# Gated linear attention with experts: output transposes and k transposes at other places in TensorE's order

## The chip, the core and the metric

The kernel runs on one core of one Trainium2 chip. The metric is the device time of one execution in microseconds. Three runs of the kernel before are shown; the changed kernel is compared with it on the same chip.

## The reference

Sixteen sequences of 512 tokens with 256 features go through an attention block and then a feed-forward block with eight experts, each with a layer norm before it, another behind it and a residual:

```
q, k = heads(x@Wq) * HK**-0.5, heads(x@Wk);  v = heads(x@Wv)     # 4 heads, HK = 64, HV = 128
g = log_sigmoid(x@gk_w1@gk_w2 + gk_b) / 16
S = exp(g_t)[:, None] * S + k_t[:, None] * v_t[None, :];  o_t = q_t @ S     # scan over tokens
o = o * rsqrt(mean(o*o) + eps) * rms_w * silu(x@Wg);  return o @ Wo
x = x + layernorm(attn(layernorm(x)))
x = x + layernorm(gelu(layernorm(x)@w1[e] + b1[e]) @ w2[e] + b2[e])          # expert e = sequence // 2
```

## The kernel before

The scan is done in four chunks of 128 tokens (`NCH`). Within a chunk, seven levels of pairwise products (`level`, `top_level`, lines 274 to 308) fill the chunk's attention matrix `Am`; between chunks a state `S` is carried. Projections run as three products of fp32r parts (hi x hi, hi x lo, lo x hi: `three`, lines 262 to 272); transposes, state products and attention products are plain fp32.

The program is a loop over sequences. `run(s, j, e, B, C, A)` does three things in one turn, interleaved by hand: stage B is the attention of sequence s, C is the feed-forward block of sequence p = s - 1, A (with V) is the layer norm, the transposes and the projections of sequence n = s + 1. There is a first fill, a first turn without C, fourteen turns with all three, a turn without A, and a last one with C alone. Each engine has its own copy of this loop and works off its instructions in the order in which they are written; semaphores tie the engines together. So the order inside `run` on each engine is what counts.

The steps of TensorE that the change touches, with `c` for the chunk:
- `xt` transposes the normed x of sequence n into the banks `PT[0]`, `PT[1]`; `x_hi` (ScalarE) and a `lo_part` (VectorE) split them to `xT_hi`, `xT_lo`.
- `kh(f)` (line 389) transposes `k_decayed`, six 128x128 blocks in all, into `PT[f]`; ScalarE copies them to `kT` (`ac_kt`).
- `f2(c)` (line 378) is the second feed-forward product, 24 passes for one chunk; `gd` and `gl` are the products of the gate of sequence n; `kp`, `qp`, `vp(c)`, `gp(c)` are the projections to k, q, v and output gate, each three passes over each half of the features, 6 in all. `vp(1)` waits until ScalarE has copied `v` of chunk 0 (`v_evac(0)`).
- `st(c)` (line 486) is k^T v of a chunk into the bank `PS`; `att(c)` (line 502) is the chunk's output into `PO`, from `Am` and, past the first chunk, from the state.
- `ogt(c)` (line 520) transposes the gated output `o` of a chunk, four blocks, into `PT[c % 2]`. `og_hi(c)` (ScalarE) and `og_lo(c)` (VectorE, line 763) split it to `ogT_hi`, `ogT_lo`. `wo(c)` (line 530), 12 passes, multiplies by Wo into `PL[c % 2]` and needs both.

Between `att(c)` and `ogt(c)` lies a chain over three engines: `o_evac(c)` copies `PO` to `o` (ScalarE), `squares(c)` sums its squares by head (ScalarE, eight short instructions), `o_rstd(c)` takes the reciprocal root (POOL, lines 1384 and 1387), `og(c)` multiplies by it and by the gate (VectorE, line 756).

Three ends of the order matter. TensorE: `ogt(0)` stands between `vp(0, n)` and `gp(0, n)`, `ogt(1)` between `vp(1, n)` and `wo(0)`. VectorE: `og_lo(0)`, `og(1)`, `state(2)`. ScalarE: `squares(1)`, `og_hi(0)`, `v_evac(0, n)`, `o_evac(2)`. In the trace, line 279 is `transpose_tokens`, 398 `kh`, 430 and 432 `gd`, 497 `st`, 513 and 516 `att`, 527 `ogt`, 269 to 271 the three passes of `three`, 693 `lo_part`, 751 `state`, 760 `og`.

Of the kernel before, what the change touches and what calls it, by code (L numbers as in the profile page):

```python
# [21 lines left out]
def build(nc, x_d, wq_d, wk_d, wv_d, wg_d, w1g_d, w2g_d, gkb_d, wo_d, rms_d,  # L22
# [6 lines left out]
    P = 128  # L29
# [9 lines left out]
    KT = D // P  # L39
# [12 lines left out]
    with ctx:  # L52
# [133 lines left out]
        def at(name, b, c):  # L186

            return b * PER[name] + c
# [74 lines left out]
        def _(pe):  # L263
# [19 lines left out]
            def run(s, j, e, B, C, A):  # L283
# [92 lines left out]
                def f2(c):  # L376
                    pe.wait_ge(sem["po_w2"], at("po_w2", e, 8))
                    if c >= 2:
                        pe.wait_ge(sem["dv_y4"], at("dv_y4", p, c - 1))
                    else:  # L380
                        pe.wait_ge(sem["ac_gelu"], at("ac_gelu", p, FT - 1 + c))
                    t = slice(c * CH, (c + 1) * CH)
                    for m in range(FT):
                        pe.wait_ge(sem["dv_hlo"], at("dv_hlo", p, m + 1))
                        last = three(PB[c % 2][:, 0:D], [(h_hi[:, m, t], h_lo[:, m, t])],
                                     [(W2[0][:, m, :], W2[1][:, m, :])], m == 0, m == FT - 1)
                    last.then_inc(sem["pe_f2"], 1)

                def kh(f):
                    pe.wait_ge(sem["po_ku"], at("po_ku", s, 2 * (NL - 1)))  # L390
                    if A:
                        pe.wait_ge(sem["dv_xlo"], at("dv_xlo", n, f + 1))
                    elif C:
                        pe.wait_ge(sem["dv_hlo"], at("dv_hlo", p, FT - 1 + f))
                    for c in range(2 - f):
                        for tl in range(KT):
                            w = (2 * f + c) * CH
                            last = nc.tensor.transpose(PT[f][:, c * D + tl * P:c * D + (tl + 1) * P],
                                                       kk[:, tl, w:w + CH], ident[:, :])
                    last.then_inc(sem["pe_kt"], 1)  # L400

# [57 lines left out]
                def vp(c, b):  # L459
                    if c == 0 and b == 0:  # L460
                        pe.wait_ge(c_lo, 2)
                        pe.wait_ge(sem["k_sb"], at("k_sb", b, 1))
                    elif c == 0:
                        pe.wait_ge(sem["k_sb"], at("k_sb", b, 1))
                    elif c == 1 and b == 0:
                        pe.wait_ge(sem["dv_gl"], at("dv_gl", b, KT))
                        pe.wait_ge(sem["ac_abs"], at("ac_abs", b, KT))
                    elif c == 2:
                        pe.wait_ge(sem["dv_q"], at("dv_q", b, 2 if b else 4))
                    else:  # L470
                        pe.wait_ge(sem["v_sb"], at("v_sb", b, c))
                    token_tile(PL[0] if c == 1 and b == 0 else PB[0], c, 0).then_inc(sem["pe_v"], 1)

                def gp(c, b):
                    if c == 0 and b == 0:
                        pe.wait_ge(c_lo, 3)
                        pe.wait_ge(sem["dv_q"], at("dv_q", b, 4))
                    elif c == 0:
                        pe.wait_ge(sem["k_sb"], at("k_sb", b, 2))
                    elif c == 2 and b:  # L480
                        pe.wait_ge(sem["dv_q"], at("dv_q", b, 4))
                    else:
                        pe.wait_ge(sem["ac_g"], at("ac_g", b, c))
                    token_tile(PB[1], c, 1).then_inc(sem["pe_g"], 1)

                def st(c):

                    pe.wait_ge(sem["ac_kt"], at("ac_kt", s, c // 2 + 1))
                    pe.wait_ge(sem["v_sb"], at("v_sb", s, c + 1))
                    if c:  # L490
                        pe.wait_ge(sem["dv_st"], at("dv_st", s, states(c)))
                    elif C:
                        pe.wait_ge(sem["dv_st"], at("dv_st", p, states(NCH - 1)))
                    for tl in range(KT):
                        for hh in range(2):
                            hd = 2 * tl + hh
                            last = nc.tensor.matmul(PS[hh * HK:(hh + 1) * HK, tl * HV:(tl + 1) * HV],
                                                    kT[:, c, hd * HK:(hd + 1) * HK],
                                                    v[:, c, hd * HV:(hd + 1) * HV], start=True, stop=True)
                    last.then_inc(sem["pe_st"], 1)  # L500
# [19 lines left out]
                def ogt(c):  # L520
                    pe.wait_ge(sem["dv_og"], at("dv_og", s, H * (c + 1)))
                    if c >= 2:
                        pe.wait_ge(sem["dv_oglo"], at("dv_oglo", s, c - 1))
                    else:
                        pe.wait_ge(sem["ac_kt"], at("ac_kt", s, c + 1))
                    for k in range(VT):
                        last = nc.tensor.transpose(PT[c % 2][:, k * P:(k + 1) * P], o[:, c % 2, k * P:(k + 1) * P], ident[:, :])  # L527
                    last.then_inc(sem["pe_ogt"], 1)

                def wo(c):  # L530
                    if not C:
                        pe.wait_ge(c_lo, 4)
                    pe.wait_ge(sem["dv_oglo"], at("dv_oglo", s, c + 1))
                    if c < 2 and A:
                        pe.wait_ge(sem["dv_gl"], at("dv_gl", n, KT))
                    if c >= 2:
                        pe.wait_ge(sem["dv_t"], at("dv_t", s, c - 1))
                    else:
                        pe.wait_ge(sem["ac_cp"], at("ac_cp", s, 8 + 2 * (c + 1)))
                    three(PL[c % 2][:, 0:D], [(ogT_hi[:, k, :], ogT_lo[:, k, :]) for k in range(VT)],  # L540
                          [(WO[0][:, k, :], WO[1][:, k, :]) for k in range(VT)]).then_inc(sem["pe_wo"], 1)
# [59 lines left out]
                if V and C:  # L601
                    xt(0)
                    xt(1)
                if C:
                    f2(3)
                if B:
                    kh(0)
                    kh(1)
                if A:
                    gd()  # L610
                if B:
# [10 lines left out]
                    att(1)  # L622
                if V:
                    vp(0, n)
                if B:
                    ogt(0)
                if V:
                    gp(0, n)
                if B:
                    st(2)  # L630
                    att(2)
                if V:
                    vp(1, n)
                if B:
                    ogt(1)
                    wo(0)
                    att(3)
                    wo(1)
                if V:
# [30 lines left out]
        def _(dve):  # L670
# [17 lines left out]
            def run(s, j, e, B, C, A):  # L688
# [74 lines left out]
                def og_lo(c):  # L763
                    lo_part(ogT_lo[:, :, :], ogT_hi[:, :, :],
                            PT[c % 2][:, :].rearrange("p (k t) -> p k t", k=VT), "ac_oghi", s, c + 1, "dv_oglo")
# [196 lines left out]
                if A:  # L962
                    gate_sub()
                if B:
                    og_lo(0)
                    og(1)
                    state(2)
                    ln2(0)
                    og_lo(1)
                    og(2)  # L970
                    normed_attn(0)
                    ln2(1)
                    og_lo(2)
                    og(3)
                    normed_attn(1)
# [24 lines left out]
        def _(act):  # L1000
# [21 lines left out]
            def run(s, j, e, B, C, A):  # L1022
# [3 lines left out]
                def copy(dst, src, name):  # L1026
                    nc.scalar.activation(dst, src, ACT.Copy).then_inc(sem[name], 1)  # L1027
# [102 lines left out]
                def og_hi(c):  # L1130
                    act.wait_ge(sem["pe_ogt"], at("pe_ogt", s, c + 1))
                    if c:
                        act.wait_ge(sem["pe_wo"], at("pe_wo", s, c))
                    copy(ogT_hi[:, :, :], PT[c % 2][:, :].rearrange("p (k t) -> p k t", k=VT), "ac_oghi")
# [68 lines left out]
                if B:  # L1203
                    for f in range(2):
                        act.wait_ge(sem["pe_kt"], at("pe_kt", s, f + 1))
                        copy(kT[:, 2 * f:NCH - 1 if f else 2, :].rearrange("p c d -> p (c d)"), PT[f][:, 0:(2 - f) * D], "ac_kt")
                    if not C:
                        expand(1)
                if A:
# [17 lines left out]
                    o_evac(1)  # L1227
                if B:
                    squares(1)
                    og_hi(0)  # L1230
                if V:
                    v_evac(0, n)
                if B:
                    o_evac(2)
                if A:
                    act.wait_ge(sem["dv_gsub"], at("dv_gsub", n, 1))
# [256 lines left out]
```

## Time and profile before

| | us |
|---|---|
| median of 3 runs (lowest, highest) | 1144.31 (1144.15, 1145.76) |
| the profiled execution, in all | 1146.42 |
| its span, first to last instruction | 1144.6 |
| TensorE matmuls in flight, of the span | 1104.1 (96%) |
| TensorE weight loads | 911.4 (80%) |
| VectorE | 870.8 (76%) |
| ScalarE | 812.3 (71%) |
| GpSimd (POOL) | 598.3 (52%) |
| mean granted TensorE clock, share of full | 0.99 |

Busy times of the engines overlap. A row of a timeline has the start in us from the span's start, how long it took, engine, line, output and inputs, and how many instructions were merged; brackets at the end give the idle time of the engine before it and what released it. A matmul's duration holds its way through the array, so its rate is read from start to start.

### The profile page before, as it was taken

What the parts mean: (1) busy time and instruction counts of PE and PEld (TensorE: products, weight loads), DVE (VectorE), ACT (ScalarE), POOL (GpSimd) and SP (SyncE); (2) the same over time, 40 slices, a digit from 0 to 9 for tenths busy, and PEclk for the clock granted to TensorE, in tenths of its full rate; (3) what the DMA queues carried; (4) which work ended last, traced back from release to release, by engine and by line L of the source; (5) the groups of instructions that cost most, each with busy time, mean ns of one, the idle gap of its engine ahead of it and who ended that gap; (6) DMA issues with size and microseconds to landing.
All of it is one profiled execution on the core that took longest, in us unless ns stands there. A gap on an engine that the chain in (4) does not pass through costs nothing.

```text
span 1144.6 us, 32286 instructions
## 1 busy us (share of the span) xinstructions
PE 1104.1 (96%) x12624; PEld 911.4 (80%) x12624; DVE 870.8 (76%) x2009; ACT 812.3 (71%) x1748; POOL 598.3 (52%) x907
## 2 busy tenths in 40 slices
PE   5899999999999999999999999999999999999967
PEld 4687878888788888878888788887878888788857
DVE  7669587785877868687786967869587785877763
ACT  5687767778687687867778676787767778687533
POOL 7645445464456643564455635645445464456631
PEclk9899999999999999999999999999999999999989
DMA  4000012000110001200102001010012000120000
GB/s 154 18 23 21 19 58 61 20 3 19 58 61 21 17 5 57 61 20 20 56 3 61 21 20 57 19 44 21 20 58 61 20 3 19 58 61 2 21 1 19
DMA packets 32966, 38.89 MB, mean 34 GB/s; under 512 B 3568, under 2 KB 30256, under 8 KB 32816
## 3 DMA queue, kind: packets, MB, share of 16 engines
q1 hardware_dynamic: 32240, 36.30, 9.7%
q8 instruction: 102, 1.67, 0.6%
q10 hardware_dynamic: 576, 0.52, 0.2%
q14 instruction: 48, 0.39, 0.1%
HBM read 28.43 MB, written 8.39 MB: 32 GB/s over the span
## 4 chain that ended last, share of the span: by engine, by line
PE 66%; ACT 16%; DVE 11%; issue 6%; POOL 0%; DMA 0%; SPq 0%; DVEq 0%; POOLq 0%; ACTq 0%
PE ps_big L269 15%; PE ps_big L270 12%; PE ps_big L271 12%; DVE q_blockdiag L724 4%; PE ps_level L330 3%; PE ps_level L269 3%; ACT square_out L1094 3%; PE ps_out L513 3%; PE ps_transpose L279 3%; PE ps_level L271 3%; PE ps_level L270 3%; DVE h_lo L737 2%; PE ps_transpose L527 2%; ACT L1222 2%; PE ps_out L516 1%
## 5 line engine op out<-in xcount | busy, mean ns | idle before, releaser
L1366 POOL TENSOR_TENSOR k_decayed<-k_decayed,block_totals 128x256 f32<-128x256 f32 x192 | 144.2, 768 | 178.1 <-PE ps_level L330 127.9
L724 DVE TENSOR_TENSOR q_blockdiag<-q_blockdiag,block_totals 128x512 f32<-128x512 f32 x192 | 174.6, 923 | 3.2 <-PE ps_level L308 3.2
L269 PE MATMUL ps_big<-w_ff_hi,h_hi 128*128 128x256 f32 x512 | 150.6, 294 | 1.9 <-DVE h_lo L737 1.4
L270 PE MATMUL ps_big<-w_ff_lo,h_hi 128*128 128x256 f32 x512 | 144.6, 282 | 0.0
L271 PE MATMUL ps_big<-w_ff_hi,h_lo 128*128 128x256 f32 x512 | 144.6, 282 | 0.0
L1372 POOL TENSOR_TENSOR rstd<-mean_var,minus_half 128x1 f32<-128x1 f32 x192 | 106.8, 574 | 51.8 <-DVE mean_var L771 51.1
L1035 ACT ACTIVATE ps_transpose<-ps_big,ff_b_cols 128x512 f32<-128x512 f32 x128 | 84.7, 661 | 51.4 <-DVE h_lo L737 32.2
L1027 ACT ACTIVATE h_hi<-ps_transpose 128x512 fp32r<-128x512 f32 x160 | 94.1, 598 | 32.8 <-PE ps_transpose L279 16.9
L269 PE MATMUL ps_big<-h_hi,w_ff_hi 128*128 128x512 f32 x256 | 110.0, 430 | 1.9 <-DVE h_lo L693 1.4
L269 PE MATMUL ps_big<-w_vg_hi,xT_hi 128*128 128x512 f32 x254 | 109.8, 432 | 0.8
L737 DVE TENSOR_TENSOR h_lo<-ps_transpose,h_hi 128x512 fp32r<-128x512 f32 x128 | 84.3, 681 | 34.2 <-ACT h_hi L1027 34.2
L1396 POOL TENSOR_TENSOR w_ff_lo<-w_raw,w_ff_hi 128x256 fp32r<-128x256 f32 (+1 forms) x96 | 104.3, 1104 | 0.0
L269 PEld LDWEIGHTS ps_big<-w_ff_hi,h_hi 128*128 128x128 f32 x512 | 97.7, 191 | 7.6 <-DVE h_lo L737 5.1
L270 PE MATMUL ps_big<-h_lo,w_ff_hi 128*128 128x512 f32 x256 | 101.5, 396 | 0.0
L271 PE MATMUL ps_big<-h_hi,w_ff_lo 128*128 128x512 f32 x256 | 101.5, 396 | 0.0
L270 PE MATMUL ps_big<-w_vg_lo,xT_hi 128*128 128x512 f32 x254 | 100.5, 396 | 0.0
L271 PE MATMUL ps_big<-w_vg_hi,xT_lo 128*128 128x512 f32 x254 | 100.5, 396 | 0.0
L270 PEld LDWEIGHTS ps_big<-w_ff_lo,h_hi 128*128 128x128 f32 x512 | 97.9, 191 | 0.0
L271 PEld LDWEIGHTS ps_big<-w_ff_hi,h_lo 128*128 128x128 f32 x512 | 97.8, 191 | 0.0
L513 PE MATMUL ps_out<-v,attn_T 128*128 128x128 f32 x512 | 95.8, 284 | 0.0
L1384 POOL TENSOR_SCALAR o_rstd<-o_sumsq 128x4 f32<-128x4 f32 x64 | 12.4, 193 | 156.5 <-ACT square_out L1094 156.5
L330 PEld LDWEIGHTS ps_level<-q_blockdiag,k_decayed 128*32 128x32 f32 x5120 | 57.0, 112 | 40.9 <-issue 20.4
(157 smaller groups left out, 3129.1 us busy)
## 6 DMA issues: line engine op xcount, KB each, us to landing
w_raw<-L_ffn_w SPq DMA_DIRECT2D x16, 1024.0 KB, 6.0
out<-y SPq DMA_DIRECT2D x64, 128.0 KB, 1.7
x_in<-L_attn_x SPq DMA_DIRECT2D x15, 512.0 KB, 3.9
ff_b_rows<-L_ffn_b SPq DMA_DIRECT2D x8, 128.0 KB, 2.3
x_in<-L_attn_x ACTq DMA_DIRECT2D x4, 128.0 KB, 2.7
w_raw<-L_attn_Wv SPq DMA_DIRECT2D x1, 512.0 KB, 4.5
w_raw<-L_attn_Wg SPq DMA_DIRECT2D x1, 512.0 KB, 6.4
y<-L_attn_Wo SPq DMA_DIRECT2D x1, 512.0 KB, 7.4
```

Source lines behind the costliest of these rows:

```text
L269: nc.tensor.matmul(out, ah, bh, start=(first and i == 0), stop=False)
L270: nc.tensor.matmul(out, ah, bl, start=False, stop=False)
L271: last = nc.tensor.matmul(out, al, bh, start=False, stop=(final and i == n - 1))
L330: last = nc.tensor.matmul(PL[tl][BS * g:BS * (g + 1), c * BS:(c + 1) * BS], kk[:, tl, t], q[:, :, :, 1, :], start=True, stop=True)
L513: last = nc.tensor.matmul(PO[:, w], Am[:, tl, 2 * c + hh, :], v[:, c, w], start=True, stop=(c == 0))
L724: nc.vector.tensor_tensor(q, q, t.to_broadcast([P, 2, T // (2 * h), h]), ALU.mult)\
L737: nc.vector.tensor_tensor(h_lo[:, m, :], PT[m % 2][:, :], h_hi[:, m, :].bitcast(F32), ALU.subtract).then_inc(sem["dv_hlo"], 1)
L1027: nc.scalar.activation(dst, src, ACT.Copy).then_inc(sem[name], 1)
L1035: nc.scalar.activation(PT[m % 2][:, :], PB[m % 2][:, :], ACT.Gelu_apprx_tanh, bias=b1s[:, m:m + 1]).then_inc(sem["ac_gelu"], 1)
L1366: nc.gpsimd.tensor_tensor(k, k, t.to_broadcast([P, m, h]), ALU.mult)\
L1372: nc.gpsimd.tensor_tensor(rs[:, k, c:c + 1], mv[:, k, c, 1:2], mhalf[:, 0:1], ALU.pow)\
L1396: nc.gpsimd.tensor_tensor(flat[1], raw[:, part * w:(part + 1) * w], flat[0].bitcast(F32), ALU.subtract).then_inc(sem[name], 1)
```

## The change

`kh(0)` and `kh(1)` move ahead of `f2(3)`, directly behind `xt`, and write to the banks `PO` and `PS` in place of `PT`; their waits change to fit, and `st` always waits for both copies to `kT`. `ogt(0)` moves behind `gp(0, n)`, next to `st(2)`; `ogt(1)` and `wo(0)` change places, so `ogt(1)` stands next to `att(3)`. `ogt(0)` and `ogt(1)` wait for `xT_lo` having been read out of `PT` instead of the copies to `kT`. On ScalarE `og_hi(0)` moves behind `v_evac(0, n)`; on VectorE `og(1)` moves ahead of `og_lo(0)`. The number of products, copies and transfers stays as it is.

```diff
--- before.py
+++ after.py
@@ -387,15 +387,15 @@
                     last.then_inc(sem["pe_f2"], 1)
 
                 def kh(f):
+                    if f == 0:
+                        pe.wait_ge(sem["dv_c0"], at("dv_c0", s, KT))
+                    elif C:
+                        pe.wait_ge(sem["dv_st"], at("dv_st", p, states(NCH - 1)))
                     pe.wait_ge(sem["po_ku"], at("po_ku", s, 2 * (NL - 1)))
-                    if A:
-                        pe.wait_ge(sem["dv_xlo"], at("dv_xlo", n, f + 1))
-                    elif C:
-                        pe.wait_ge(sem["dv_hlo"], at("dv_hlo", p, FT - 1 + f))
                     for c in range(2 - f):
                         for tl in range(KT):
                             w = (2 * f + c) * CH
-                            last = nc.tensor.transpose(PT[f][:, c * D + tl * P:c * D + (tl + 1) * P],
+                            last = nc.tensor.transpose((PO, PS)[f][:, c * D + tl * P:c * D + (tl + 1) * P],
                                                        kk[:, tl, w:w + CH], ident[:, :])
                     last.then_inc(sem["pe_kt"], 1)
 
@@ -485,7 +485,7 @@
 
                 def st(c):
 
-                    pe.wait_ge(sem["ac_kt"], at("ac_kt", s, c // 2 + 1))
+                    pe.wait_ge(sem["ac_kt"], at("ac_kt", s, 2))
                     pe.wait_ge(sem["v_sb"], at("v_sb", s, c + 1))
                     if c:
                         pe.wait_ge(sem["dv_st"], at("dv_st", s, states(c)))
@@ -521,8 +521,10 @@
                     pe.wait_ge(sem["dv_og"], at("dv_og", s, H * (c + 1)))
                     if c >= 2:
                         pe.wait_ge(sem["dv_oglo"], at("dv_oglo", s, c - 1))
-                    else:
-                        pe.wait_ge(sem["ac_kt"], at("ac_kt", s, c + 1))
+                    elif A:
+                        pe.wait_ge(sem["dv_xlo"], at("dv_xlo", n, c + 1))
+                    else:
+                        pe.wait_ge(sem["dv_hlo"], at("dv_hlo", p, FT - 1 + c))
                     for k in range(VT):
                         last = nc.tensor.transpose(PT[c % 2][:, k * P:(k + 1) * P], o[:, c % 2, k * P:(k + 1) * P], ident[:, :])
                     last.then_inc(sem["pe_ogt"], 1)
@@ -601,11 +603,11 @@
                 if V and C:
                     xt(0)
                     xt(1)
+                if B:
+                    kh(0)
+                    kh(1)
                 if C:
                     f2(3)
-                if B:
-                    kh(0)
-                    kh(1)
                 if A:
                     gd()
                 if B:
@@ -622,18 +624,16 @@
                     att(1)
                 if V:
                     vp(0, n)
+                    gp(0, n)
                 if B:
                     ogt(0)
-                if V:
-                    gp(0, n)
-                if B:
                     st(2)
                     att(2)
                 if V:
                     vp(1, n)
                 if B:
+                    wo(0)
                     ogt(1)
-                    wo(0)
                     att(3)
                     wo(1)
                 if V:
@@ -962,8 +962,8 @@
                 if A:
                     gate_sub()
                 if B:
+                    og(1)
                     og_lo(0)
-                    og(1)
                     state(2)
                     ln2(0)
                     og_lo(1)
@@ -1203,7 +1203,7 @@
                 if B:
                     for f in range(2):
                         act.wait_ge(sem["pe_kt"], at("pe_kt", s, f + 1))
-                        copy(kT[:, 2 * f:NCH - 1 if f else 2, :].rearrange("p c d -> p (c d)"), PT[f][:, 0:(2 - f) * D], "ac_kt")
+                        copy(kT[:, 2 * f:NCH - 1 if f else 2, :].rearrange("p c d -> p (c d)"), (PO, PS)[f][:, 0:(2 - f) * D], "ac_kt")
                     if not C:
                         expand(1)
                 if A:
@@ -1227,10 +1227,10 @@
                     o_evac(1)
                 if B:
                     squares(1)
-                    og_hi(0)
                 if V:
                     v_evac(0, n)
                 if B:
+                    og_hi(0)
                     o_evac(2)
                 if A:
                     act.wait_ge(sem["dv_gsub"], at("dv_gsub", n, 1))
```

## Rows read from the trace of the kernel before

**Rows 1.** the page: engine, busy us (share of the span), instructions

```profile
PE 1104.1 (96%) x12624; PEld 911.4 (80%) x12624; DVE 870.8 (76%) x2009; ACT 812.3 (71%) x1748; POOL 598.3 (52%) x907
```

**Rows 2.** waits of TensorE's matmuls: us in total, times, longest us

```profile
PE ps_level L269 <- DVE ogT_lo L693: 2.8, 2, 1.4
```

**Rows 3.** waits of TensorE's weight loads, same columns

```profile
PEld ps_big L269 <- ACT v L1027: 6.2, 30, 0.2
```

**Rows 4.** timeline, x and k transposes: start, us, engine, line, tiles, count

```profile
392.26 0.36 PE L269 MATMUL ps_big<-w_ff_hi,h_hi 128*128 128x256 f32 x1
...
392.46 0.28 PE L270 MATMUL ps_big<-w_ff_lo,h_hi 128*128 128x256 f32 x1
...
392.58 0.28 PE L271 MATMUL ps_big<-w_ff_hi,h_lo 128*128 128x256 f32 x1
...
395.21 0.82 PE L398 MATMUL ps_transpose<-ident,k_decayed 128*128 128x128 f32 x6
...
395.79 0.48 PE L430 MATMUL ps_level<-xT_hi,w_gate_down_for_hi 128*128 128x512 f32 x1
...
396.10 0.40 PE L432 MATMUL ps_level<-xT_lo,w_gate_down_for_lo 128*128 128x512 f32 x1
...
396.33 0.40 PE L430 MATMUL ps_level<-xT_hi,w_gate_down_for_hi 128*128 128x512 f32 x1
```

**Rows 5.** timeline of TensorE around the first output transposes

```profile
405.64 0.60 PE L527 MATMUL ps_transpose<-ident,o 128*128 128x128 f32 x4
...
406.00 0.48 PE L269 MATMUL ps_big<-w_vg_hi,xT_hi 128*128 128x512 f32 x1
...
406.31 0.40 PE L270 MATMUL ps_big<-w_vg_lo,xT_hi 128*128 128x512 f32 x1
```

**Rows 6.** timeline of POOL, ACT and DVE before the first output projection

```profile
409.61 1.01 POOL L1387 TENSOR_TENSOR o_rstd<-o_rstd,minus_half 128x4 f32<-128x4 f32 x1
...
409.63 0.58 ACT L1027 ACTIVATE v<-ps_big 128x512 f32<-128x512 f32 x1
...
409.76 0.69 DVE L693 TENSOR_TENSOR ogT_lo<-ps_transpose,ogT_hi 128x512 fp32r<-128x512 f32 x1 [1.05 <-ACT ogT_hi L1027]
...
410.65 1.14 DVE L760 SCALAR_TENSOR_TENSOR o<-o,o_rstd,out_gate 128x128 f32<-128x128 f32 x4 [0.20 <-POOL o_rstd L1387]
...
411.71 0.60 DVE L751 SCALAR_TENSOR_TENSOR state<-state,block_totals,ps_state 128x128 f32<-128x128 f32 x2
```

**Rows 7.** timeline, TensorE's weight loads and matmuls, and one DVE row, same turn

```profile
410.26 0.19 PEld L269 LDWEIGHTS ps_big<-w_vg_hi,xT_hi 128*128 128x128 f32 x1 [0.24 <-ACT v L1027]
...
412.26 0.36 PE L269 MATMUL ps_level<-w_o_hi,ogT_hi 128*128 128x256 f32 x1
...
413.78 0.39 PE L513 MATMUL ps_out<-v,attn_T 128*128 128x128 f32 x2
...
414.89 0.69 DVE L693 TENSOR_TENSOR ogT_lo<-ps_transpose,ogT_hi 128x512 fp32r<-128x512 f32 x1 [0.25 <-ACT ogT_hi L1027]
...
415.64 0.39 PE L269 MATMUL ps_level<-w_o_hi,ogT_hi 128*128 128x256 f32 x1
...
418.57 0.60 PE L527 MATMUL ps_transpose<-ident,o 128*128 128x128 f32 x4
...
420.60 0.37 PE L269 MATMUL ps_level<-w_o_hi,ogT_hi 128*128 128x256 f32 x1
```

**Rows 8.** timeline of the first turn around its k transposes

```profile
47.41 1.93 POOL L1366 TENSOR_TENSOR k_decayed<-k_decayed,block_totals 128x192 f32<-128x192 f32 x2 [2.05 <-PE ps_level L308]
...
49.72 1.14 PE L398 MATMUL ps_transpose<-ident,k_decayed 128*128 128x128 f32 x6 [2.41 <-DVE xT_lo L693]
```

**Rows 9.** timeline of DVE in the last of the fourteen full turns

```profile
1028.33 1.14 DVE L760 SCALAR_TENSOR_TENSOR o<-o,o_rstd,out_gate 128x128 f32<-128x128 f32 x4 [0.20 <-POOL o_rstd L1387]
```

**Rows 10.** busy us by stretch, columns PE, PEld, DVE, ACT, POOL, PEclk, DMA

```profile
51.00:54.00 3.00, 3.00 (x14) 1.83 (x13) 0.31 (x1) 2.53 (x6) 3.00 (x3) 0.52 0.00 0
...
128.60:1090.00 961.40, 953.59 (x11043) 788.17 (x11042) 746.20 (x1738) 706.23 (x1529) 506.42 (x757) 1.00 0.10 33
```

## What I expect, and why

> **What bounds the kernel now.** I read the page first: matmuls are in flight for 96% of the span [rows 1], and the table by stretches shows TensorE at its full granted clock from 128.6 to 1090 us, 953.59 of 961.40 busy [rows 10]. So nearly every stall of TensorE's queue is paid in full, and nothing that another engine saves counts unless TensorE waits for it. Then I read who TensorE waits for. In its matmul row the waits are few and short: two for `ogT_lo` together 2.8 us [rows 2]. The weight loads, which run one step ahead, show small waits that come back in every turn of the loop: for `v` 30 times, 6.2 us in all, 0.2 the longest [rows 3]. They say that TensorE arrives at such places only a little before its data does. A change of order here can therefore lose more than it gains. Last I read one turn of the loop as a timeline, from the x transposes at 391.47 us to the third output projection. The fourteen full turns repeat within a few hundredths of a microsecond; `og(1)` shows the same 0.20 us wait in the last of them [rows 9] as in the one I read [rows 6].
>
> **What a border between two kinds of products costs.** The idea that the diff allows is to have fewer borders between plain fp32 work (transposes, `st`, `att`) and the three-pass fp32r products (`f2`, `gd`, `vp`, `gp`, `wo`). I price a border by starts, since durations overlap. Inside `f2` passes of 256 columns start 0.12 apart (392.46 to 392.58), but the first pass behind the x transposes (392.26) is followed by its second only after 0.20: 0.08 more. The six k transposes take 395.21 to 395.79, 0.58, or 0.10 each, and the first `gd` pass is followed after 0.31 where later ones follow after 0.23: 0.08 again [rows 4]. Four output transposes take 405.64 to 406.00, 0.36, and the next pair starts 0.31 apart [rows 5]. So a border out of transposes into fp32r costs 0.08, and going into transposes costs nothing that shows.
>
> The Trainium skill, "TensorE: Matmul & The Clock Gate", section "Step-by-step: what each phase is for", says that TensorE pulls weight loads ahead of matmuls in flight, so that the next weights come in under the running matmul. By that a border would be free, and the 0.08 that I take off below for each turn would fall away: some 1.2 us more in the whole time, near 1152.0. The row with its 0.20 against 0.12 speaks against it, and I go by the row.
>
> **Part 1: the k transposes (`kh`) stand before `f2(3)`, in PO and PS.** The same six transposes, 0.58 us, only at another place. They now follow the x transposes without a border, so one border of 0.08 goes per turn. Their new waits: for `k_update` of the top level on POOL, for `copy_diag` and for the last turn's states. The latter two are long done. POOL ends the top level before the x transposes start in the turns that I read; in the first turn it ends at 49.34 [rows 8]. Nothing new waits. ScalarE's copies to `kT` then lie beside `f2(3)` (392.26 to 395.21, 2.95 us), so `st(0)` can wait for both at no cost. The fourth `ln4` on VectorE begins about 0.6 later because `f2(3)` ends that much later, but `gd` directly behind it is not moved, and `lowrank_lo` waits for ScalarE's copy of `gd` anyway; without that cover it would cost up to 0.2. So everything from `gd` on stands 0.08 earlier.
> In the first turn `kh` waits 2.41 us for `xT_lo` [rows 8]. That wait goes, but POOL's update, ending 49.34, comes in its place, with `kh` at about 49.40 instead of 49.72: 0.32 gained once.
>
> **Part 2: `ogt(0)` goes behind `gp(0)`, and `og_hi(0)` behind `v_evac(0)` on ScalarE.** `ogt(0)` now touches `st(2)`: one more border of 0.08 goes. A border from transposes into `st` isn't in the trace; between nothing and the 0.17 that `att` loses behind `st` I take nothing, and it is covered by the wait below in any case. `v_evac(0)` started at 409.63 behind `og_hi(0)` [rows 6], and `vp(1)` waited 0.24 for it, until 410.26 [rows 7]. Now it goes first and is done in time, and `vp(1)` starts when TensorE is there: 410.02 less the two borders of 0.16, so 409.86. It takes 1.52 (410.26 to the end of its slot at 411.78), so TensorE is through at 411.38. That is 0.4 us ahead of today.
>
> **Part 3: `wo(0)` now comes before `ogt(1)`, and on VectorE `og(1)` before `og_lo(0)`.** This decides. `wo(0)` needs `og_lo(0)`. Today that runs at 409.76, in the gap before `og(1)`, and is finished at 410.45, long before `wo(0)` starts at 412.26 [rows 6, 7]. VectorE works its queue in order. With the new order `og_lo(0)` stands behind `og(1)`, and `og(1)` can't start before POOL has the reciprocal roots: these end at 410.62, and `og(1)` starts at 410.65 [rows 6]. Behind them are the squares on ScalarE, which follow one another without a gap from `att(0)` on; the change moves that chain only by the 0.08 of part 1. So `og(1)` starts at 410.57. The instruction that follows it today, `state(2)`, starts 1.06 after it (411.71); `og_lo(0)` does so at 411.63 and takes 0.69: 412.32. TensorE starts some 0.05 after such an end (`og_lo(1)` ends 415.58, `wo(1)` starts 415.64 [rows 7]). `wo(0)` starts at 412.37, about 1.0 us after TensorE has reached it. Behind the waiting `wo(0)` in TensorE's queue are `ogt(1)`, `att(3)`, `wo(1)`: all work of the turn.
> From there: `wo(0)` takes 1.52 (412.26 to 413.78), `ogt(1)` 0.36 as the first one did, so `att(3)` starts at 414.25 instead of 413.78. It takes 1.81 (today 1.86 with 0.05 of waiting for `og_lo(1)`), so `wo(1)` starts at 416.06 instead of 415.64: 0.42 later. `og_lo(1)` is ready by then, at about 415.8.
>
> **Is the 0.42 given back later in the turn?** `ogt(2)` starts at 418.57 and `wo(2)` at 420.60 [rows 7]. Between them only `qp(0)` runs, which fills 1.5 of the 2.03, and there is 0.2 of waiting for `v_evac(1)`. But `wo(2)` waits for the chain of `ogt(2)`, `og_hi(2)` and `og_lo(2)`, which starts from TensorE's own transpose, so this slack doesn't take up a late start. The same holds for `wo(3)`, and the rest of the turn is TensorE-bound. I take the whole 0.42.
>
> **The sum.** Fourteen full turns of 0.42 are 5.9. The first turn: 0.42 less 0.32, 0.1. The last turn has no input stage; the same exchange of `og(1)` and `og_lo(0)` holds there, with a gain before it of about 0.1: 0.4. Together 6.4. The profiled execution spans 1144.6 and took 1146.42 with what lies around it; it becomes 1151.0 of span and 1152.8 in all. The median of the three runs is 1144.31, which is 2.1 below the profiled one, so the forecast for the median is 1150.7. Bounds per turn: 0.34, if `wo(0)` after its wait starts without the 0.08 of a first pass; 0.68, if `og_lo(0)` doesn't overlap the end of `og(1)` (0.08) and `att(3)` loses 0.17 behind transposes. That is 1149.5 to 1154.7 with the first and the last turn. Half a microsecond for the last turn is added on both sides: 1149.0 to 1155.2.
>
> **Rivals.**
> *The borders win (faster).* Three borders go per turn, and the weight loads sit idle before `st` for up to 0.35. If each of the three costs 0.08 out of fp32 and 0.09 in, and `wo(0)` doesn't wait, 16 turns gain 16 x 3 x 0.17, 8.2: 1136.1; with the 0.08 alone, 3.8: 1140.5. It decides this way if `og(1)` could start before about 409.6, so that `og_lo(0)` is done when TensorE arrives at 411.38. Against it: POOL's end at 410.62, in every turn. 7 in 100, at 1140.
> *The wait is there but is taken up (no change).* If 0.3 or more of the lag disappears in the waits for `v_evac(1)` or `og_lo(1)`, each turn loses at most 0.1, 1144 to 1146. For it: the loads' waits of [rows 3] are slack of this kind. Against it: the two that come behind hang on TensorE's own transposes. 12 in 100.
> *The wait costs the clock.* One microsecond of idle in each turn could lower the granted clock. In the first turn the wait of 2.41 us [rows 8] is followed by a stretch, 51 to 54 us, whose granted clock is 0.52 [rows 10], the level of 1.2 GHz. If such 3 us came in each turn, they would hold half as much work: 1.5 us more a turn, up to 21 in all, 1157 to 1172. The new wait is less than half as long as that one, and the small waits of today lower nothing, so 4 in 100.
> *The change of order does nothing at the place.* If the program's waits made TensorE go through `ogt(1)` first as before, only part 1 would count, 1.3 less: 1143. This is in the no-change case, 2 more in 100.
>
> **How the numbers follow.** Forecast 75 in 100, the faster rival 7, taken up or nothing 14, clock 4. A measurement of this kernel can tell about 0.2% from no change, 2.3 us, so 1142.0 to 1146.6 is the same. Slower 0.78, same 0.14, faster 0.08. The forecast's own range is 1149.0 to 1155.2 and holds it about 9 times in 10, so 68 in 100; to reach 8 in 10 I go down into the case where the lag is taken up in part: 1145.8 to 1155.2.
>
> **What would show it.** In the profile after, in each turn: `wo(0)`'s first pass with a wait for `ogT_lo` of about 1 us, a group that is to show 15 or 16 waits where it shows two; `og_lo(0)` directly behind `og(1)`, about 1.06 after its start; `vp(1)` without its wait; the fourteen turns each 0.4 longer from one `gd` to the next; `kh` directly behind the x transposes, and `gd`'s first pass followed after 0.23. Wrong would be: no wait before `wo(0)`, an `og(1)` that starts earlier than 14.8 after `gd` (410.57 less 395.79), or turns that are shorter.

## The result and the profile after

The changed kernel takes 1151.38 us in the median of five runs, 1151.18 to 1153.67; the kernel before took 1145.76 on the same chip, 1144.15 to 1146.71. The medians stand 5.6 us apart; the ratio over all five runs of each is 1.006, with a 95% interval of 1.0049 to 1.0072. The forecast was 1150.7 for a kernel before of 1144.31, 6.4 us more and a ratio of 1.0056. The ratios in this document leave out one execution, of the third experiment's kernel, that took 2070.51 us at the full granted clock, for a reason that no trace here shows.

The page of the profile after, its span and first section, shows the loss as time that TensorE does not have work in flight. Its busy time fell by 6.7 us against [rows 1] while the span grew from 1144.6 to 1150.8:

```profile
span 1150.8 us, 32285 instructions
...
PE 1097.4 (95%) x12624; PEld 910.7 (79%) x12624; DVE 870.0 (76%) x2009; ACT 813.0 (71%) x1748; POOL 600.0 (52%) x907
```

The waits of TensorE's matmuls (us in total, times, longest) say for what. The row of [rows 2] has gone from 2 waits to 17, from 2.8 us to 16.2 (the wait is about twice the loss, since TensorE also reaches `wo(0)` earlier than before); the wait of the first turn's k transposes for `xT_lo` [rows 8] has become one for POOL:

```profile
PE ps_level L269 <- DVE ogT_lo L693: 16.2, 17, 1.5
...
PE ps_out L398 <- POOL k_decayed L1366: 2.2, 1, 2.2
```

The same turn stretch as in [rows 6, 7], in a turn whose `gd` starts at 465.74 (line 529 is `ogt` now). Start, us, engine, line, tiles, count, idle before:

```profile
476.90 0.60 PE L529 MATMUL ps_transpose<-ident,o 128*128 128x128 f32 x4
...
477.43 0.66 PE L497 MATMUL ps_state<-v,k_tokens 128*64 128x128 f32 x8
...
479.02 0.57 ACT L1027 ACTIVATE v<-ps_big 128x512 f32<-128x512 f32 x1
...
479.48 1.01 POOL L1387 TENSOR_TENSOR o_rstd<-o_rstd,minus_half 128x4 f32<-128x4 f32 x1
...
479.83 0.48 PE L269 MATMUL ps_big<-w_vg_hi,xT_hi 128*128 128x512 f32 x1
...
480.53 1.14 DVE L760 SCALAR_TENSOR_TENSOR o<-o,o_rstd,out_gate 128x128 f32<-128x128 f32 x4 [1.95 <-POOL o_rstd L1387]
...
481.59 0.68 DVE L693 TENSOR_TENSOR ogT_lo<-ps_transpose,ogT_hi 128x512 fp32r<-128x512 f32 x1
...
482.33 0.39 PE L269 MATMUL ps_level<-w_o_hi,ogT_hi 128*128 128x256 f32 x1 [0.85 <-DVE ogT_lo L693]
...
483.85 0.60 PE L529 MATMUL ps_transpose<-ident,o 128*128 128x128 f32 x4
...
484.28 0.39 PE L513 MATMUL ps_out<-v,attn_T 128*128 128x128 f32 x2
...
485.11 0.69 DVE L693 TENSOR_TENSOR ogT_lo<-ps_transpose,ogT_hi 128x512 fp32r<-128x512 f32 x1 [0.40 <-ACT ogT_hi L1027]
...
485.99 0.36 PE L269 MATMUL ps_level<-w_o_hi,ogT_hi 128*128 128x256 f32 x1
```

`v` is copied first, so `vp(1)` (479.83) starts without a wait. `og(1)` starts right behind POOL, `og_lo(0)` follows it 1.06 us after its start and ends at 482.27, and `wo(0)` starts 0.06 later. `vp(1)` was through at 481.35 (479.83 and 1.52), so TensorE stood for 0.98 us by starts; the row's 0.85 counts from the modelled end of the last matmul. From there the steps follow without a wait: `ogt(1)` 1.52 after `wo(0)`, `att(3)` 0.43 later, `wo(1)` at 485.99.

The length of a turn is read from the first `gd` matmul to the next turn's. Before and after, the turn of the same parity:

```profile
464.11 0.48 PE L430 MATMUL ps_level<-xT_hi,w_gate_down_for_hi 128*128 128x512 f32 x1
...
533.12 0.48 PE L430 MATMUL ps_level<-xT_hi,w_gate_down_for_hi 128*128 128x512 f32 x1
```

```profile
465.74 0.40 PE L430 MATMUL ps_level<-xT_hi,w_gate_down_for_hi 128*128 128x512 f32 x1
...
535.24 0.40 PE L430 MATMUL ps_level<-xT_hi,w_gate_down_for_hi 128*128 128x512 f32 x1
```

That is 69.01 before and 69.50 after; every other turn is shorter, and those went from 68.32 to 68.77. In each kernel turns of one kind agree within 0.1 us (one turn of the seventh experiment, 68.43 among 68.27 to 68.31, is the exception), so the turn is a far finer measure than the whole time, and the experiments are read by it.

### The profile page after: what moved, and what is told of

It reads as the page before. It is cut to its first block and busy times, and to the rows that moved or that the text cites. A ratio compares the mean times of both kernels' runs of the same rounds, so it can differ in the third digit from the quotient of the medians.

```text
span 1150.8 us, 32285 instructions
## 1 busy us (share of the span) xinstructions
PE 1097.4 (95%) x12624; PEld 910.7 (79%) x12624; DVE 870.0 (76%) x2009; ACT 813.0 (71%) x1748; POOL 600.0 (52%) x907
## 5 line engine op out<-in xcount | busy, mean ns | idle before, releaser
L760 DVE SCALAR_TENSOR_TENSOR o<-o,o_rstd,out_gate 128x128 f32<-128x128 f32 x256 | 75.4, 357 | 39.4 <-POOL o_rstd L1387 39.3
L269 PE MATMUL ps_level<-w_o_hi,ogT_hi 128*128 128x256 f32 x256 | 78.5, 307 | 19.0 <-DVE ogT_lo L693 16.2
```

The lines of the kernel that those rows point to most:

```text
L269: nc.tensor.matmul(out, ah, bh, start=(first and i == 0), stop=False)
L760: nc.vector.scalar_tensor_tensor(o[:, c % 2, w], o[:, c % 2, w], rso[:, c * H + hd:c * H + hd + 1], gs[:, c, w], ALU.mult, ALU.mult).then_ ...
```

## Experiments

The turn lengths of all kernels, from the differences between successive first `gd` matmuls (medians of the seven shorter and the six longer ones), and where `wo(0)` and `wo(1)` start after `gd`, us, in the median. Each ratio is taken against runs of the kernel before on the same chip (medians 1144.23 for the first four, 1144.40 for the fifth to the eighth, 1145.07 for the ninth). A kernel with one run has its time in place of a ratio; one time can't be told from before within some 2 us, so these kernels are read by their turns alone.

| kernel | turns | wo(0) | wo(1) | ratio to before (95%) |
|---|---|---|---|---|
| before | 68.32, 69.03 | 16.48 | 19.85 | |
| changed | 68.77, 69.50 | 16.59 | 20.25 | 1.006 (1.0049 to 1.0072) |
| e1_kh_only | 68.29, 69.02 | 16.39 | 19.78 | 1.0005 (0.9994 to 1.0015) |
| e2_og_lo_back | 68.29, 69.03 | 15.57 | 19.77 | 0.999 (0.9982 to 0.9999) |
| e3_wo_back | 68.33, 69.06 | 16.58 | 19.83 | 1.0008 (0.9999 to 1.0018) |
| e4_short_root | 68.56, 69.30 | 16.36 | 20.04 | 1.0034 (1.0022 to 1.0046) |
| e5_swap_only | 68.30, 69.04 | 16.67 | 19.91 | one run, 1144.69 |
| e6_v1_ahead | 68.41, 69.15 | 15.57 | 19.77 | one run, 1144.46 |
| e7_v0_on_vector | 68.30, 69.00 | 15.57 | 19.77 | one run, 1143.28 |
| e8_v0_and_exp | 67.80, 68.51 | 15.56 | 19.28 | 0.9913 (0.99 to 0.9927) |
| e9_before_v0_exp | 68.13, 68.82 | 16.48 | 19.70 | 0.9976 (0.9966 to 0.9985) |

The theory: the loss is the wait for `og_lo(0)`, which stands behind `og(1)` on VectorE. Rivals: the moved transposes cost time by their place or banks; the two swapped steps on TensorE cost it by themselves; the loss lies in ScalarE's new order.

**The k transposes alone (e1_kh_only).** All of part 1 in the kernel before, among it:

```diff
-                if C:
-                    f2(3)
                 if B:
                     kh(0)
                     kh(1)
+                if C:
+                    f2(3)
                 if A:
                     gd()
```

> The kernel before with part 1 alone: the k transposes ahead of f2(3), in the banks PO and PS; output transposes, wo and the other engines as before. The forecast took 0.08 us per turn for the border that goes and 0.3 once in the first turn: 1.6 us less than before, ratio 0.9986. A look at the trace of the changed kernel says that a border is worth about nothing (the transposes are only as long as their own spacing of 0.107 us): then only the first turn gains, ratio 0.9995 to 1.000. Rival, that the k transposes in their new place and banks carry part of the 5.6 us lost: ratio above 1.001.

Turns are 0.01 to 0.03 shorter than before and the ratio can't be told from 1. The k transposes carry nothing of the loss, and the border that I priced at 0.08 is worth 0.03 or less.

**VectorE's old order in the changed kernel (e2_og_lo_back).**

```diff
                 if B:
-                    og(1)
                     og_lo(0)
+                    og(1)
                     state(2)
```

> The changed kernel with og_lo(0) ahead of og(1) on VectorE again, all else as changed. Order theory: wo(0) finds its input at 15.1 us after gd and no longer waits when TensorE reaches it at 15.6; the next bound is og_lo(1), which waits for the squares on ScalarE, so wo(1) starts at 19.8 after gd instead of 20.25, as in the kernel before. Time as before: ratio 0.999 to 1.001, turns of 68.3 and 69.0 us. Rival, that the moved transposes themselves (their place and banks on TensorE) cost the 0.45 us a turn: ratio stays 1.004 to 1.006.

This one edit takes the whole loss away. The moved transposes and their banks, the swapped steps on TensorE and the new order on ScalarE are all still there, so none of them costs it by itself. Timeline of VectorE, TensorE and one row of ScalarE in a turn whose `gd` starts at 532.57:

```profile
546.94 0.69 DVE L693 TENSOR_TENSOR ogT_lo<-ps_transpose,ogT_hi 128x512 fp32r<-128x512 f32 x1 [1.53 <-ACT ogT_hi L1027]
...
547.55 1.13 DVE L760 SCALAR_TENSOR_TENSOR o<-o,o_rstd,out_gate 128x128 f32<-128x128 f32 x4
...
548.14 0.28 PE L269 MATMUL ps_level<-w_o_hi,ogT_hi 128*128 128x256 f32 x1
...
550.99 0.57 ACT L1027 ACTIVATE ogT_hi<-ps_transpose 128x512 fp32r<-128x512 f32 x1
...
551.59 0.69 DVE L693 TENSOR_TENSOR ogT_lo<-ps_transpose,ogT_hi 128x512 fp32r<-128x512 f32 x1 [1.16 <-ACT ogT_hi L1027]
...
552.34 0.38 PE L269 MATMUL ps_level<-w_o_hi,ogT_hi 128*128 128x256 f32 x1 [0.38 <-DVE ogT_lo L693]
```

`og_lo(0)` runs at 546.94 in front of `og(1)`, and `wo(0)` starts at 548.14, straight behind `vp(1)`, a microsecond earlier than in the changed kernel (15.57 against 16.59 after `gd`). Yet the turn is only as short as before: `wo(1)` waits until 552.34 for `og_lo(1)`. It starts at 19.77, as expected, and the microsecond is lost again. So a second bound lay right behind the first.

**TensorE's old order at wo(0) and ogt(1) (e3_wo_back).**

```diff
                 if B:
-                    wo(0)
                     ogt(1)
+                    wo(0)
                     att(3)
```

> The changed kernel with ogt(1) ahead of wo(0) on TensorE again, og_lo(0) still behind og(1) on VectorE. Order theory: wo(0) starts at 16.6 after gd as in the changed kernel, since og_lo(0) sets it, but ogt(1) is already done, so att(3) follows 0.43 us earlier and wo(1) starts at 19.93 instead of 20.25: 0.3 us less a turn than the changed kernel, 0.15 more than before, ratio 1.0015 to 1.003. If the wait for og_lo(0) were not the cause but the two swapped steps, ratio near 1.000.

`wo(0)` starts at 16.58 as predicted, so VectorE's order sets it here too. The turns came out 0.43 to 0.44 shorter than in the changed kernel where 0.3 was expected, since `wo(1)` starts at 19.83, 0.10 earlier than I worked out; so the ratio, 1.0008, is below the 1.0015 to 1.003 that I gave. TensorE now waits at `ogt(1)`:

```profile
PE ps_transpose L529 <- DVE o L760: 5.0, 17, 0.9
...
PE ps_level L269 <- DVE ogT_lo L693: 2.8, 2, 1.4
```

**VectorE's new order alone in the kernel before (e5_swap_only).** The reverse of the edit of the second experiment, with nothing else changed.

> The kernel before with one edit: og(1) ahead of og_lo(0) on VectorE, TensorE's order untouched. Order theory: og_lo(0) is late in this order whatever TensorE does, so wo(0) starts at about 16.65 after gd instead of 16.47; ogt(1) is done ahead of it, so the loss is only 0.1 to 0.2 at att(3), and part of it disappears in the wait for og_lo(1): turns 0.05 to 0.15 us longer than 68.32 and 69.02. If the loss came from VectorE's order alone, turns would be 0.45 longer.

`wo(0)` starts 0.19 later (16.67) and `wo(1)` 0.06 later, but the turns stay within 0.02 of before, where I had expected 0.05 to 0.15 more. With the second and the third experiment this shows that the loss needs both halves: `og_lo(0)` behind `og(1)`, and `wo(0)` ahead of `ogt(1)`. One half alone costs at most 0.04 us a turn.

**A shorter chain to `og` (e4_short_root).**

```diff
-                    nc.gpsimd.tensor_scalar(rso[:, w], ssq[:, w], 1.0 / HV, EPS, ALU.mult, ALU.add)\
-                        .then_inc(sem["po_ro"], 1)
-                    pool.wait_ge(sem["po_ro"], at("po_ro", s, 2 * c + 1))
-                    nc.gpsimd.tensor_tensor(rso[:, w], rso[:, w], mhalf[:, w], ALU.pow)\
-                        .then_inc(sem["po_ro"], 1)
+                    nc.gpsimd.tensor_tensor(rso[:, w], ssq[:, w], mhalf[:, w], ALU.pow)\
+                        .then_inc(sem["po_ro"], 2)
```

> The changed kernel with a shorter chain to og: POOL takes the power straight from the sum of squares; the multiplication by 1/128 and the addition of epsilon are left out, so the outputs differ in scale before the layer norm. This takes 0.28 us (0.19 and the step between) from the chain that ends in og_lo(0). Order theory: the wait before wo(0) shrinks by 0.28 and each turn by 0.23 to 0.28, 3.4 to 4.2 us in all: ratio to before 1.0020 to 1.0030. If the loss is on TensorE or ScalarE and not in this chain, ratio stays 1.005 to 1.006.

This kernel leaves out the factor 1/128 and the epsilon; it serves only to shorten the chain. Cutting POOL's part moves `og(1)` by 0.22 (14.57 after `gd` instead of 14.79), `wo(0)` by as much, the turn by 0.20 to 0.21. The row of `wo(0)` shows the wait at 0.60 where the changed kernel has 0.85:

```profile
547.27 1.14 DVE L760 SCALAR_TENSOR_TENSOR o<-o,o_rstd,out_gate 128x128 f32<-128x128 f32 x4 [1.73 <-POOL o_rstd L1384]
...
549.07 0.38 PE L269 MATMUL ps_level<-w_o_hi,ogT_hi 128*128 128x256 f32 x1 [0.60 <-DVE ogT_lo L693]
```

The ratio, 1.0034, lies just above the 1.0020 to 1.0030 that I gave, in part since the step was worth 0.22 and not 0.28; its interval, 1.0022 to 1.0046, reaches into that range. The loss follows the length of the chain almost one for one, which ties it to the chain by another way than the order.

**What is the second bound?** In the second experiment `wo(1)` hangs on ScalarE: squares of chunk 2, `og_hi(1)` (the row at 550.99, which shows no idle time before it), then `og_lo(1)`. Three kernels start from there. First, `v_evac(1)` ahead of `squares(3)` (e6_v1_ahead).

> The kernel of the second experiment (og_lo(0) back ahead of og(1)) with v_evac(1) ahead of squares(3) on ScalarE. It takes away the small wait of qp(0) for v: qp(0) starts about 0.15 us earlier. The forecast held that this slack is not to be had, since wo(2) hangs on the chain of the output transposes: then wo(2) stays at 24.75 after gd and the turns at 68.28 and 69.02. If the wait for v was real time, turns are 0.15 shorter.

```diff
                     o_evac(3)
-                    squares(3)
                 if V:
                     v_evac(1, n)
                 if B:
+                    squares(3)
                     og_hi(2)
```

`wo(2)` starts at 24.72 against 24.74, so the small wait for `v` was no time to be had, as the forecast had it. But the turns are 0.1 longer: `wo(3)` moves from 28.37 to 28.48, since the squares of chunk 3 now end 0.33 later and `og(3)` behind them. That loss I had not expected.

The copy of `v`'s chunk 0 on VectorE (e7_v0_on_vector):

> The kernel of the second experiment with the copy of v's chunk 0 moved from ScalarE to VectorE, where it falls into a gap. ScalarE has 0.57 us less to do ahead of the squares of chunk 2. Theory: ScalarE's chain to og_lo(1) now sets wo(1), but its next step, o_evac(2), waits for att(2) on TensorE anyway (about 14.35 after gd), so nothing is gained: turns within 0.05 of 68.28 and 69.02. Rival, that the chain is short of plain ScalarE time: turns 0.4 to 0.57 shorter.

```diff
+                if V:
+                    v_copy(0, n)
                 if A:
                     gate_sub()
```

with `v_copy` a `tensor_copy` of the same bank on VectorE, and `v_evac(0, n)` gone from ScalarE. Nothing is gained: 68.30 and 69.00. The time that ScalarE no longer needs for the copy it now spends waiting for `att(2)`, as the row of `o_evac(2)` shows:

```profile
545.29 0.60 ACT L1035 ACTIVATE o<-ps_out 128x512 f32<-128x512 f32 x1 [0.55 <-PE ps_out L516]
```

The same, and the exponential of the gates ahead of `o_evac(2)` (e8_v0_and_exp):

> As the seventh, and ScalarE does the exponential of the gates before o_evac(2) instead of after it. Now the freed 0.57 us falls where ScalarE would wait for att(2): the squares of chunk 2 end at about 18.0 after gd instead of 18.45, og_lo(1) and wo(1) follow at 19.35 instead of 19.77, and all behind it. Turns 0.35 to 0.45 shorter than before, 5 to 7 us in all: ratio 0.994 to 0.9955. If the bound at wo(1) is not ScalarE's chain: ratio 0.999 to 1.000.

```diff
                 if B:
                     og_hi(0)
-                    o_evac(2)
                 if A:
                     act.wait_ge(sem["dv_gsub"], at("dv_gsub", n, 1))
                     nc.scalar.activation(ga[:, :, :], gm[:, :, :], ACT.Exp, scale=1.0 / GATE_NORM)\
                         .then_inc(sem["ac_a"], 1)
                 if B:
+                    o_evac(2)
                     squares(2)
```

ScalarE, VectorE and TensorE in a turn of this kernel whose `gd` starts at 526.52:

```profile
536.50 0.69 DVE L771 COPY v<-ps_big 128x512 f32<-128x512 f32 x1 [0.72 <-PE ps_big L271]
...
540.39 1.28 ACT L1242 ACT_TABLE_LOAD   x1
...
541.68 1.06 ACT L1242 ACTIVATE gates<-gate_and_q 128x1024 f32<-128x1024 f32 x1
...
542.11 0.28 PE L269 MATMUL ps_level<-w_o_hi,ogT_hi 128*128 128x256 f32 x1
...
542.65 0.58 ACT L1035 ACTIVATE o<-ps_out 128x512 f32<-128x512 f32 x1
...
544.45 0.57 ACT L1035 ACTIVATE ogT_hi<-ps_transpose 128x512 fp32r<-128x512 f32 x1
...
545.05 0.69 DVE L694 TENSOR_TENSOR ogT_lo<-ps_transpose,ogT_hi 128x512 fp32r<-128x512 f32 x1 [0.64 <-ACT ogT_hi L1035]
...
545.79 0.39 PE L269 MATMUL ps_level<-w_o_hi,ogT_hi 128*128 128x256 f32 x1
```

ScalarE loads the table and does the exponential where in the seventh experiment it had to wait for `att(2)`, `og_hi(1)` starts at 544.45, and `wo(1)` at 545.79, 19.27 after `gd`: 0.08 earlier than expected. Turns are 0.5 us shorter than before, so ScalarE's chain was the second bound. The exponential was not moved without the copy, so what it would give alone is not shown. The time is 1134.66 (1134.09 to 1136.37) beside 1144.40 of before: a ratio of 0.9913, better than both kernels and than the 0.994 that I had expected at best. Of the 9.7 us the traces put 6.65 into the thirteen distances between the `gd` of the full turns. In the profiles the first turn is also 0.88 shorter, the stretch behind the last `gd` 1.50 shorter, and the second `gd` comes 2.66 earlier; how much of these three is the edit isn't shown, since the start and the stretch behind differ by such amounts between kernels with the same turns (129.23 to 131.59 us behind the last `gd` in the second and the fifth experiment; for the start see below).

The two edits without the change (e9_before_v0_exp):

> The kernel before, with TensorE's order untouched, and with the two edits of the eighth experiment alone: the copy of v's chunk 0 on VectorE, the exponential of the gates before o_evac(2). Theory: in the order of before, ogt(1) stands ahead of wo(0) and waits for og(1) until 16.05 after gd, so att(3) starts at 18.0 and wo(1) at 19.8 by TensorE's own work; the earlier og_lo(1) finds nobody waiting. Turns 0.0 to 0.1 shorter than 68.32 and 69.02, ratio 0.998 to 1.000. Then the new order of TensorE is what the eighth kernel's gain needs. Rival, that the two edits alone make the gain: turns 0.4 to 0.5 shorter, ratio 0.991 to 0.994.

The same two edits in TensorE's old order give 0.19 to 0.21 a turn, twice what I allowed, and 0.9976, just below the 0.998 that I gave. `wo(0)` stays at 16.48, held by `ogt(1)`, which waits for `og(1)`:

```profile
544.13 1.14 DVE L761 SCALAR_TENSOR_TENSOR o<-o,o_rstd,out_gate 128x128 f32<-128x128 f32 x4 [0.20 <-POOL o_rstd L1392]
...
545.33 0.66 PE L527 MATMUL ps_transpose<-ident,o 128*128 128x128 f32 x4 [0.24 <-DVE o L761]
...
545.74 0.36 PE L269 MATMUL ps_level<-w_o_hi,ogT_hi 128*128 128x256 f32 x1
```

So of the 0.52 in the eighth kernel 0.3 needs what the change brings on TensorE, with `og_lo(0)` left where it was. The two kernels differ in TensorE's order and the banks of `kh` alone, and the k transposes are worth 0.03 at most (first experiment). Of what is left, the new place of `ogt(0)` and the exchange of `wo(0)` and `ogt(1)`, neither was tried by itself; the wait of `ogt(1)` in front of `wo(0)` points to the exchange.

## Why the prediction was right, point by point

- *The new wait before `wo(0)`.* Right, with its place, size and cause. Expected 1.0 us, 0.98 by starts; `og(1)` 14.78 after `gd`, measured 14.79; `og_lo(0)` 1.06 behind its start, measured 1.06; `wo(0)` at 16.58 (412.37 less 395.79), measured 16.59. The second, third, fourth and fifth experiments tie the loss to it.
- *`wo(1)` and what is given back.* `wo(1)` expected at 20.27 after `gd`, measured 20.25. The lag was kept to the end of the turn; turns are 0.45 to 0.47 longer where the sum had 0.42. Between the two starts luck helped: `ogt(1)` takes 0.43 and not 0.36, `att(3)` 1.71 and not 1.81 (483.85, 484.28 and 485.99), and the two misses all but cancel. The refusal of the slack at `wo(2)` was right too (sixth experiment).
- *The price of a border, 0.08 (the second paragraph of the forecast): wrong.* In the changed kernel the x and k transposes stand together:

```profile
530.84 1.03 PE L279 MATMUL ps_transpose<-ident,x_normed 128*128 128x128 f32 x8
...
531.71 0.60 PE L398 MATMUL ps_out<-ident,k_decayed 128*128 128x128 f32 x4
...
532.15 0.38 PE L398 MATMUL ps_state<-ident,k_decayed 128*128 128x128 f32 x2
...
532.29 0.36 PE L269 MATMUL ps_big<-w_ff_hi,h_hi 128*128 128x256 f32 x1
...
532.49 0.28 PE L270 MATMUL ps_big<-w_ff_lo,h_hi 128*128 128x256 f32 x1
```

Eight x transposes take 0.87 (530.84 to 531.71) when others follow, not the 0.79 (459.79 to 460.58 in the rows of before, below) ahead of an `f2` pass. That pass starts 0.08 early, while the last transposes are still in flight, and its second pass then comes 0.08 late: I had counted only the late half. From 530.84 to the second pass at 532.49 are 1.65 us for 14 transposes and one pass of 0.12, so 0.109 per transpose; before, eight of them and the pass took 1.00 (459.79 to 460.79), 0.110 each:

```profile
459.79 1.03 PE L279 MATMUL ps_transpose<-ident,x_normed 128*128 128x128 f32 x8
...
460.58 0.36 PE L269 MATMUL ps_big<-w_ff_hi,h_hi 128*128 128x256 f32 x1
...
460.79 0.28 PE L270 MATMUL ps_big<-w_ff_lo,h_hi 128*128 128x256 f32 x1
```

The six k transposes of [rows 4] say the same: from 395.21 to the second `gd` pass at 396.10 are 0.89, six at 0.109 and one pass of 0.23; the 0.58, or 0.10 each, that I read was cut short by the early start of the pass. So a border between transposes and fp32r products is free, within the 0.03 of the first experiment. The trace agrees with the rule of the Trainium skill, "TensorE: Matmul & The Clock Gate", section "Step-by-step: what each phase is for", that I had weighed and set aside; by it the sum gave 1152.0. So the 0.08 of part 1 and that of part 2 fall out of the sum. The second was covered by the wait anyway; the first is the greater part of why a turn lost 0.45 to 0.47 and not 0.42.
- *The total: close in part by luck.* The spans differ by 6.2 us where the sum had 6.4. The thirteen distances from the first `gd` of the full turns to that of the last one with an input stage lost 5.95 (the sum: 5.5), the stretch behind them 0.83 (0.8). The first turn is 0.58 longer from its `gd` on, and that `gd` comes 1.19 earlier, of which 0.80 was there before the k transposes and has nothing to do with the change: 0.2 lost once these are taken off, where the sum had 0.1. So the change costs about 7 in these traces (the granted clock from 51 to 54 us differs too, 0.52 before and 0.72 after, so the first turn is no exact measure), and an early start of this one execution hides the difference. In the medians the loss is 5.6, and the absolute 1150.7 lies near 1151.38 partly because the kernel before came out at 1145.76 this time and not at 1144.31.
- *Two slips in the sums.* 0.42, 0.08 and 0.17 are 0.67 a turn, not 0.68; and part 1 alone was worth 1.6 by its own terms, not the 1.3 of the last rival. Neither moves the forecast.
- *The border of `ogt(0)`.* `ogt(0)` beside `st(2)` gained nothing either: 476.90 to 477.43 is 0.53, four transposes and the 0.1 that a step into `st` cost before as well (`gp(0)`'s last pass to `st(2)` takes 0.33, where passes follow one another after 0.23).
- *The first turn.* The wait for POOL took the place of the wait for `xT_lo`, 2.2 us for 2.41, as said; `kh` starts 0.1 behind POOL's end.
- *The clock.* It stayed at its full level: over 128.6 to 1090 us the granted clock is 1.00 before and after, so a microsecond of standing still a turn lowers nothing here. The clock rival had leaned on the 0.52 behind the first turn's wait. In the first and the eighth experiment the same place has a wait of 2.2 us too, and the granted clock from 51 to 54 us is 1.00; so that wait by itself does not lower it.

## What to carry to other kernels

Before a step is moved on the engine that bounds, write down for the new place when TensorE arrives and when each input is there, and follow the input back through the queues of the other engines: here following one start, `og_lo(0)`, gave those of `wo(0)` and `wo(1)` to 0.02 us. When two orders are changed together, on TensorE and on VectorE, try each half alone: here either half cost 0.04 us a turn at most, and the pair lost 0.45 to 0.47. The half on TensorE was even worth keeping, once ScalarE's chain was shorter. And when a wait is taken away and nothing gets faster, look for the next engine whose chain ends at the same place.

## What the runs showed of the hardware

Between a run of transposes and fp32r products a matmul pass starts early by as much as the next one comes late; only the distance over both, or a kernel with the border removed, gives the price: 0.01 to 0.03 us a turn.

The turns repeat within 0.1 us, but whole times of one kernel spread over 1.1 us (1142.99 to 1144.10 in the second experiment) to 4.4 us (1141.98 to 1146.34 in the first). Much of this goes with the granted clock. Of the thirty executions of the kernel before that stand beside the first four experiments, the six with a mean clock of 0.994 took 1142.42 to 1142.62, the eleven with 0.992 or 0.993 took 1143.35 to 1144.28, and the ten with 0.990 took 1144.92 to 1146.41. In the traces the clock differs in the first 60 us. In the kernel before it has a dip (0.83 and 0.89), in the profile of the eighth experiment, the second pair of rows, none. By stretch: length, busy of PE, PEld, DVE, ACT, POOL, then PEclk, DMA share, GB/s.

```profile
25.00:45.00 20.00, 16.58 (x405) 12.49 (x406) 17.34 (x33) 12.30 (x20) 12.73 (x18) 0.83 0.02 4
...
45.00:60.00 15.00, 12.23 (x102) 9.43 (x101) 7.89 (x14) 12.52 (x34) 8.41 (x9) 0.89 0.23 71
```

```profile
25.00:45.00 20.00, 16.07 (x445) 12.29 (x445) 17.81 (x34) 13.94 (x27) 13.30 (x17) 1.00 0.01 4
...
45.00:60.00 15.00, 11.83 (x83) 9.61 (x77) 7.67 (x15) 13.47 (x30) 8.06 (x8) 1.00 0.22 71
```

The second `gd` then starts at 47.85 instead of 50.51. Over the eleven profiles it starts at 47.35 to 48.21 where the granted clock from 25 to 45 us is 1.00 (four), at 48.61 to 48.88 where it is 0.91 (three) and at 49.32 to 50.51 where it is 0.83 (four). What decides on the dip was not tried.
